# Attention stage: the values' way from PSUM to the output projection, by transposes or by DRAM scratch

## The reference, cut to what matters

```python
qkv = x @ w_qkv.T * hid ** (-0.5)          # 16 heads of 16 channels, 1024 tokens
scores = jnp.einsum('bhqd,bhkd->bhqk', q, k) * d ** (-0.5)
attn = jax.nn.softmax(scores, axis=-1) * (s / np.sqrt(s - 1.0))
out = jnp.einsum('bhqk,bhkd->bhqd', attn, v) * s ** (-0.5)
return out @ w_o.T * hid ** (-0.5)
```

## Time and profile before

| what | value |
|---|---|
| median of 3 runs | 5788.56 us (5783.28 to 5793.2) |
| profiled execution | 5800.13 us, span 5798.4 us |
| busy: TensorE, VectorE, ScalarE, GpSimd | 94%, 78%, 60%, 27% |
| pairs in the attention stage | 128, from about 2111 to 4832 us |
| DMA in the stage | 58 GB/s, 17.8% of 16 engines |

### The profile page before, as it was taken

How to read it: one execution, slowest core, us unless ns; L and a number is a source line. 1 busy time by engine, 2 the same in 40 slices (tenths; PEclk the granted TensorE clock), 3 DMA queues, 4 the chain that set the end, 5 groups by cost and what they waited for, 6 DMA issues and landing times. The chain is left out here.

```text
span 5798.4 us, 130675 instructions
## 1 busy us (share of the span) xinstructions
PE 5424.4 (94%) x50016; PEld 3657.9 (63%) x50016; DVE 4495.1 (78%) x7377; ACT 3471.6 (60%) x5278; POOL 1559.4 (27%) x2076
## 2 busy tenths in 40 slices
PE   7999757999989979999999999999999997799999
PEld 6777546999978834444444444444444444699998
DVE  6888676555547779999999999999999995755554
ACT  4555453333324548888888888888888886433332
POOL 5777544333320000111111111111111113533332
PEclk9999878999999979999999999999999998999999
DMA  1111292222218921111111111111111113222221
GB/s 51 51 51 51 72 275 97 95 86 87 85 62 313 332 96 47 60 58 58 57 58 60 58 58 57 58 60 57 58 57 58 60 51 100 77 89 85 95 93 49
DMA packets 315520, 495.78 MB, mean 86 GB/s; under 512 B 36314, under 2 KB 221028, under 8 KB 311024
## 3 DMA queue, kind: packets, MB, share of 16 engines
q1 hardware_dynamic: 289736, 424.67, 22.9%
q0 software_dynamic: 24576, 64.56, 3.4%
q10 hardware_dynamic: 808, 1.07, 0.1%
HBM read 321.82 MB, written 168.82 MB: 85 GB/s over the span
## 5 line engine op out<-in xcount | busy, mean ns | idle before, releaser
L1751 DVE TENSOR_REDUCE at_best<-at_psM 128x2 f32<-128x1024 f32 x2048 | 2431.6, 1222 | 225.1 <-PE at_psM L1808 212.0
L1707 ACT ACTIVATE at_p<-at_psE 128x1024 f32<-128x1024 f32 (+1 forms) x2688 | 2077.5, 824 | 527.8 <-PE at_psE L1824 514.1
L1824 PE MATMUL at_psE<-at_q,at_k 50*128 50x512 f32 x4096 | 1173.4, 436 | 7.6 <-ACT at_p L1707 6.4
L1808 PE MATMUL at_psM<-at_k,at_q 48*128 48x512 f32 x4096 | 1092.6, 458 | 37.2 <-DMA at_k<-scratch_qk 27.1
L1835 PE MATMUL at_psO<-at_p,at_v 128*17 128x256 f32 x16384 | 1109.1, 383 | 0.1
L1107 ACT ACTIVATE e_h_hi<-e_psH 128x512 fp32r<-128x512 f32 x512 | 306.6, 599 | 919.5 <-PE e_psH L90 770.2
L1824 PEld LDWEIGHTS at_psE<-at_q,at_k 50*128 50x128 f32 x4096 | 548.0, 185 | 462.4 <-issue 225.0
L1181 DVE SCALAR_TENSOR_TENSOR e_h_lo<-e_psH,e_h_hi 128x512 fp32r<-128x512 f32 x512 | 354.1, 692 | 601.7 <-ACT e_h_hi L1107 527.2
L1835 PEld LDWEIGHTS at_psO<-at_p,at_v 128*17 128x17 f32 x16384 | 364.0, 96 | 542.1 <-issue 349.2
L1808 PEld LDWEIGHTS at_psM<-at_k,at_q 48*128 48x128 f32 x4096 | 471.4, 185 | 312.5 <-DVE at_best L1751 146.4
L90 PE MATMUL e_psE<-e_w_hi,e_h_hi 128*128 128x256 f32 x2048 | 582.5, 284 | 0.0
(11 more groups left out here) (210 smaller groups left out, 8376.4 us busy)
## 6 DMA issues: line engine op xcount, KB each, us to landing
e_w_raw<-in_w SPq DMA_DIRECT2D x64, 1024.0 KB
scratch_qk<-cp_qkh SPq DMA_DIRECT2D x64, 512.0 KB
scratch_qk<-cp_qkl SPq DMA_DIRECT2D x64, 512.0 KB
at_q<-scratch_qk SPq DMA_DIRECT2D x256, 128.0 KB
at_k<-scratch_qk SPq DMA_DIRECT2D x252, 128.0 KB
scratch_v<-cp_va SPq DMA_DIRECT2D x32, 544.0 KB
at_v<-scratch_v SPq DMA_DIRECT2D x126, 136.0 KB, 9.6
a_x<-in_x SPq DMA_DIRECT2D x32, 512.0 KB
```

What stands on the lines that cost most here:

```text
L1707: nc.scalar.activation(P[:, u:u + n, :], src, ACT.Exp, scale=HD ** -0.5).then_inc(p_ready, 1)
L1751: nc.vector.reduce_max(best[j % 2][:, h, :, qt], psM[h][:], AX_X).then_inc(m_taken, 1)
L1808: last = nc.tensor.matmul(psM[h][:, a, :], Q[j][r, 128 * qt:128 * qt + 128], K[j][r, 512 * h:512 * h + 512], start=True, stop=True)
L1824: last = nc.tensor.matmul(psE[:, u - u0 if n == 2 else 2, :], K[j][r, 128 * kc:128 * kc + 128], Q[j][r, 512 * half:512 * half + 512], star ...
```

## The change

The values stay with channels on partitions. ScalarE's copy `OT` is stored to DRAM scratch `ot`; a unit of 128 channels x 256 tokens is read back from it, and its sums are read back beside it, each repeated over the 16 channels of its head. VectorE takes the reciprocal of all 128 x 256, GpSimd multiplies and splits as before. The six transposes a pair, the copy of `turn_out` and the normalising are gone. TensorE's order, `MAX_AT` (13) and VectorE's place (`INVERT_AT = 10`, after query 10) are new. The unit inverted in pair pp is loaded in pair pp, and there SyncE issues it after `load_pair`. The last batch's second half takes the same way with buffers of its own. x and the output are addressed in another order of the same tiles.

```diff
-        OUT_AT, MAX_AT, VALUES_AT, NORM_AT = 1, 11, 3, 3
+        OUT_AT, MAX_AT, VALUES_AT, INVERT_AT = 1, 13, 3, 10
+    rows = ot.rearrange("(b k i) a (m w) c -> b k m (i a) w c", k=2, i=4, m=4)
...
+            def store_values(p):
+                sp.wait_ge(oT_ready, p + 1)
+                sp.dma_start(ot[p].rearrange("a r c -> r a c"), OT[:].rearrange("r (a c) -> r a c", a=2)).then_inc(oT_stored, 16)
+            def load_unit(u, slot, b, k, m, needed):
+                sp.wait_ge(oT_stored, 16 * needed)
+                after(sp, ofT_ready, u - 1)
+                sp.dma_start(raw[slot][:], rows[b, k, m][:, 0:HD, :]).then_inc(unit_loaded[slot], 16)
+                sp.dma_start(den[slot][:], rows[b, k, m][:, HD:HD + 1, :].broadcast_to([8, HD, 256])).then_inc(unit_loaded[slot], 16)
...
                     load_pair(pp + 3, (pb + 3) % 4)
+                if not first(pp):
+                    store_values(pp - 1)
+                if has_turned(pp):
+                    u, k, m = turned_unit(pp, pb)
+                    load_unit(u, pb % 2, b if pb >= 4 else b - 1, k, m, PB * b + 4 if pb >= 4 else PB * b)
                 if there(pp + 1):
                     load_max(pp + 1, (pb + 1) % 4)
...
+            store_values(NP - 1)
+            sp.wait_ge(oT_stored, 16 * NP)
+            for m in range(4):
+                span = slice(256 * m, 256 * m + 256)
+                sp.dma_start(end_den[:, span], rows[B - 1, 1, m][:, HD:HD + 1, :].broadcast_to([8, HD, 256])).then_inc(end_loaded[m], 16)
+                sp.dma_start(end_raw[:, span], rows[B - 1, 1, m][:, 0:HD, :]).then_inc(end_loaded[m], 16)
...
             def split_out(u, slot, k, m, b):
-                pool.wait_ge(xo_taken, u + 1)
+                pool.wait_ge(rden_ready, u + 1)
+                after(pool, xo_lo_ready, u - 1)
+                nc.gpsimd.tensor_tensor(oT[slot][:], raw[slot][:], den[slot][:], ALU.mult).then_inc(ofT_ready, 1)
+                pool.wait_ge(ofT_ready, u + 1)
...
             def take_values(p):
-                after(act, t_done, p)
+                after(act, oT_stored, 16 * p)
-            def take_out(u, slot, bank):
-                nc.scalar.activation(oT[slot][:], bank[:, 128:384], ACT.Copy).then_inc(xo_taken, 1)
...
-            def normalise(p, pb, b):
+            def invert(u, slot):
+                dve.wait_ge(unit_loaded[slot], 32 * (u // 2 + 1))
+                nc.vector.reciprocal(den[slot][:], den[slot][:]).then_inc(rden_ready, 1)
+            def divide_end(m):
+                nc.vector.reciprocal(end_den[:, span], end_den[:, span]).then_inc(end_rden_ready, 1)
+                nc.vector.tensor_tensor(end_raw[:, span], end_raw[:, span], end_den[:, span], ALU.mult).then_inc(end_oT_ready, 1)
...
-                        if 2 * i + h == NORM_AT and not first(pp):
-                            normalise(pp - 1, (pb - 1) % PB, b if pb > 0 else b - 1)
+                        if 2 * i + h == INVERT_AT and has_turned(pp):
+                            invert(pp - 4, pb % 2)
...
-            def turn_values(p):
-            def turn_out(k, m, needed, bank):
...
+                output(), query(0, -1), key(0), query(1, 0), last_values(6)
+                query(2, 0), key(1), key(2), last_values(7)
+                key(3), query(3, 3), query(4, 3), key(4), values(pp, pb % 4, 0)
+                key(5), key(6), query(5, 6), values(pp, pb % 4, 1, (0,))
+                key(7), query(6, 7), key(8), values(pp, pb % 4, 1, (1,))
+                query(7, 8), key(9), query(8, 9), key(10), values(pp, pb % 4, 2)
+                key(11), query(9, 11), key(12), query(10, 12), next_max_rows(), values(pp, pb % 4, 3, (0,))
+                query(11, 12), key(13), key(14), values(pp, pb % 4, 3, (1,))
                 values(pp, pb % 4, 4, (0,)), key(15), query(12, 15), key(16), values(pp, pb % 4, 4, (1,))
+                key(17), query(13, 17), key(18), query(14, 18), key(19), values(pp, pb % 4, 5)
                 key(20), query(15, 20)
```

More of the change, by code:

```diff
@@ L1455, in _, with attention_stage @@
             groups(pe, NG, group)
-def attention_stage(nc, T, stage, x, qk, v, woT, out):
+def attention_stage(nc, T, stage, x, qk, v, ot, woT, out):
     N, D = x.shape
@@ L1486, in attention_stage @@
         OT = sb("oT", [128, 512], F32)
-        rden = sb("rden", [128, 2, KC], F32)
-        O = sb("o", [128, KC, D], F32)
+        raw = [sb(f"raw{s}", [128, 256], F32) for s in range(2)]
+        den = [sb(f"den{s}", [128, 256], F32) for s in range(2)]
+        end_raw = sb("end_raw", [128, S], F32)
+        end_den = sb("end_den", [128, S], F32)
         oT = [sb(f"ofT{s}", [128, 256], F32) for s in range(2)]
@@ L1599, in load_x @@
             def load_x(b, n):
-                sp.dma_start(X[n][:], row(xb, b)[n // 4, n % 4]).then_inc(x_loaded[n], 16)
+                sp.dma_start(X[n][:], row(xb, b)[n]).then_inc(x_loaded[n], 16)
             def store_out(u, b, n):
@@ L1756, in maximum @@
                                             best[j % 2][:, 1].rearrange("p a q -> p (a q)"), ALU.max).then_inc(mx_ready, 1)
-            def normalise(p, pb, b):
[L1760 to L1767, removed]
+            def invert(u, slot):
+                dve.wait_ge(unit_loaded[slot], 32 * (u // 2 + 1))
+                nc.vector.reciprocal(den[slot][:], den[slot][:]).then_inc(rden_ready, 1)
+            def divide_end(m):
+                span = slice(256 * m, 256 * m + 256)
+                dve.wait_ge(end_loaded[m], 32)
+                nc.vector.reciprocal(end_den[:, span], end_den[:, span]).then_inc(end_rden_ready, 1)
+                dve.wait_ge(end_rden_ready, m + 1)
+                nc.vector.tensor_tensor(end_raw[:, span], end_raw[:, span], end_den[:, span], ALU.mult).then_inc(end_oT_ready, 1)
             for j in range(4):
@@ L1830, in values @@
                 if kc == 0 and heads[0] == 0:
-                    after(pe, o_ready, pp)
+                    after(pe, oT_ready, pp)
                     pe.wait_ge(v_loaded[j], 16 * (pp // 4) + 16)
@@ L1901, in output, with next_max_rows @@
                         project_out(ub, n, psE[:, 2, :])
-                def turns():
+                def next_max_rows():
                     pe.wait_ge(p_ready, NG * pp + MAX_AT - 1)
-                    if has_turned(pp):
-                        u, k, m = turned_unit(pp, pb)
-                        turn_out(k, m, PB * b + 4 if pb >= 4 else PB * b, psE[:, 2, :])
                     if there(pp + 1):
                         max_rows(pp + 1, (pb + 1) % 4)
[L1912 to L1921, removed]
+                output(), query(0, -1), key(0), query(1, 0), last_values(6)
[6 more added lines that the diff above has]
+                query(11, 12), key(13), key(14), values(pp, pb % 4, 3, (1,))
                 values(pp, pb % 4, 4, (0,)), key(15), query(12, 15), key(16), values(pp, pb % 4, 4, (1,))
-                key(17), query(13, 17), query(14, 17), key(18), key(19), values(pp, pb % 4, 5)
+                key(17), query(13, 17), key(18), query(14, 18), key(19), values(pp, pb % 4, 5)
                 key(20), query(15, 20)
@@ L1929, in _ @@
             project_out(B - 2, PB - 1, psE[:, 0, :])
[L1930 to L1933, removed]
             for n in range(PB):
@@ L1955, in hybrid_kernel @@
         projection_stage(nc, T, "cp", x1, wqkv_bT, qk, v)
-        attention_stage(nc, T, "at", x1, qk, v, woT, out)
+        attention_stage(nc, T, "at", x1, qk, v, ot, woT, out)
         routing_stage(nc, T, R, "r2", out, wg)
```

43 lines of the change are left out of this document (20 added, 23 removed).

## The result

The changed kernel takes 7059.6 us, median of 4 runs (7048.6 to 7074.0), against 5788.2 us before: ratio 1.220, interval 1.2183 to 1.2217. The forecast was 6924 us in a range of 6450 to 7200. Of the 1271 us, 1136 had been forecast.

The account below looks back on a forecast made before the run. TensorE was taken to bound the attention stage, VectorE close behind; a late unit makes pairs 30.6 us, 9.3 more: 5800.1 + 1125 (121 pairs) + 10 = 6935, less 11.6 for the runs' median, 6924 us; range 6450 to 7200.

Parts of the forecast that it names:

- TensorE bound: Attention stage: TensorE bounds the 21.3 us pair, VectorE close behind; a long VectorE halt reaches TensorE after two tiles.
- The 32-partition loads at the head of the queue: SyncE's queue: these loads run on two of 16 DMA engines, so transfers behind land late; values load 9.6 us after issue.
- The order in SyncE's queue as the cause: The unit's store and loads, issued behind the nine loads, land at 22.5 us into the pair on average.
- The reciprocal: VectorE's new reciprocal of 256 columns, once a pair: between 0.42 and 2.3 us, taken as 1.8.
- TensorE's saving by the dropped transposes and the new order: TensorE's work per pair: net -0.7 us, so TensorE alone would need about 20.6 us.
- Rival A: The unit lands in time, no halt; with a reciprocal of 1.8 us about 21.4 us a pair, 5800 us; chance 0.12.
- Its other branch: Rival A with the reciprocal at its lower bound: 20.6 us a pair, 5712 us, faster; chance of faster 0.06.
- the clock's term: TensorE at half clock for 3.4 to 6.1 us behind each pair's halt: 1.1 to 2.3 us lost, 1.7 taken.
- 6.4 + 1.7: Per pair: 6.4 us from the unit's landing to the next output projection, plus 1.7 us for the lowered clock.
- the forecast 19.4: Values load of the nine: issued at 9.8 us into the pair, landing 9.6 us later, at 19.4.
- The end: Last batch's second half, after the last copy of sums: +8 us, and +2.4 for the other quarters; together +10.
- B: The unit is late but TensorE's clock holds: 28.9 us a pair, 6719 us; chance 0.17.

Follow-up runs that it names:

- e2: The changed kernel with each of the four loads onto 32 partitions split into two of 16 partitions, same place in the queue; 6309.8 us, ratio 1.0875.
- e3: The kernel before the change, with the four loads onto 32 partitions each split into two of 16 partitions; 5780.8 us, ratio 0.9979.
- e4: The changed kernel with only the two key loads onto 32 partitions split into loads of 16 partitions; 6622.6 us (one run), ratio 1.144.
- e1: The changed kernel with the raw values' store and the unit's two loads issued before the nine loads in SyncE's queue; 6076.9 us, ratio 1.0493.
- e6: e5 with VectorE's reciprocal over 16 of the 256 columns, the other 240 not inverted, for timing only; 5720.6 us, ratio 0.9883.
- e5: The changed kernel with the edits of e1 and e2 together; 5804.1 us, ratio 1.0027.
- e11: e5 with the reciprocal taken five times in a row, holding VectorE about 7 us longer with no transfer late; 6956.6 us (one run), ratio 1.202.

## Why the prediction was right

**The steps that held.** TensorE bound, VectorE close behind, and the two PSUM buffers passing a halt on: TensorE's 788.9 us of waits against the reciprocal's 774.7. The 32-partition loads at the head of the queue as what makes the rest land late: shown by e2, e3 and e4. The order in SyncE's queue as the cause: e1. The reciprocal: 1.8 us from the slope of the narrow ones, 1.753 measured; with 16 columns at 243 ns and 256 at 1743 (e6, e5) it is 6.25 ns a column. The upper bound of 2.3 was too high, and so was the estimate of 2.1 from the Trainium skill's page "VectorE: DVE Perf Modes" (section "Walkthrough: the 8-slice pipeline in each mode"). TensorE's saving by the dropped transposes and the new order: 0.7 us forecast, 0.6 seen between e6 and the kernel before. Rival A's sum for a unit in time, 21.4 us a pair and no change, is e5: 21.47 and 5804. Its other branch, a short reciprocal, 5712, is e6: 5721.

**The term that was too small.** The forecast had 30.6 us a pair, 31.8 were measured; 121 times 1.2 is 145, about what the sum missed. It is the clock's term: 1.7 us in the sum, 31.8 - 28.9 = 2.9 in the result. I took the stretch at half clock behind a halt from two halts of the routing stage, 3.4 and 6.1 us. Where the halt comes back every pair it is 7.9 us on average (4.0 to 12.2), and 6.0 in e11.

I also counted its cost only behind the landing. There it was right: from the reciprocal's start to the next projection it takes 8.1 us, which is 6.4 + 1.7. The missing 1.2 us lie ahead of it. The half clock reaches through the next projection to the last values of the pair before, on which SyncE waits for its loads. Those started at 4.9 us into the pair and now start at 6.1 on average (7.6 in the pair shown, 4016.86 to 4024.50). That pushes the landing back again: the values land at 20.9 instead of the forecast 19.4. The three transfers behind them needed somewhat less than I gave them, and the reciprocal starts at 23.7 instead of 22.5.

**A hit that was partly luck.** The halt of 7.2 us forecast and 7.24 measured is a difference of two times, and both came over 1 us late: VectorE wanted the unit at 16.4 us into the pair, not at 15.3, and got it at 23.7, not at 22.5. At full clock, in e5, the reciprocal does start at 15.15. The errors cancelled in the halt, but not in the pair.

**A slip.** The prediction has the nine loads "for the pair after next". They are for the pair three ahead, `load_pair(pp + 3)`. No term hangs on it.

**The end.** Forecast +10 us. From the last copy of sums to the stage's end it was 10.1 us (4831.9 to 4842.0), and is 24 (6094.2 to 6118.1), so +14. SyncE's store of the last values and the first reciprocal on them:

```profile
6094.92 0.37 SPq L1622 DMA_DIRECT2D scratch_ot<-at_oT  x1
...
6101.18 1.75 DVE L1797 RECIPROCAL at_end_den<-at_end_den 128x256 f32<-128x256 f32 x1 [16.85 <-DMA at_end_raw<-scratch_ot]
```

6.3 us from issue to reciprocal, against 8.7 forecast; what follows is longer than I had it.

**The rivals that fell.** A was never near in the changed kernel: the three transfers took the 10 us of the values load ahead of them, not the 3.6 to 3.8 of the stores. Once no 32-partition load stands in front, small transfers are quick: 2.1 us for the store of 256 KB in e1, 2.6 for the values load of 136 KB in e2. The Trainium skill's page "DMA: Bandwidth & Descriptors" (section "Anatomy of one DMA — SWDGE (gpsimd) path") has 2.0 us and bytes at 436 GB/s, stated for transfers that GpSimd issues; the estimates by it would be 2.6 and 2.3 us, near these but not equal to them. B, a clock that holds, is refuted: all five kernels of the table above with a late or held VectorE have time at half clock in the stage, and e5 has none.

## What to carry to other kernels

Read a transfer's time to landing from what is queued just ahead of it, not from others of its size later in the queue: here the same 136 KB took 10.0 us behind the four 32-partition loads and 2.6 behind their halves. Before a small, urgent transfer is added, list what needs to land by when and issue in that order: moving three issues gave back 983 of 1271 us, and the next transfer in line then became the late one. On an engine chain that is otherwise dense, as here, price a halt that recurs each iteration at its length plus the time at a lower clock behind it: here 1 to 3 us, for halts of 1.2 to 7.2 us. And ask what else starts late by it, such as the loads that wait for slowed work.

## What was not expected of the hardware

Halts of about 1.6 us a pair (e2; 3.1 in two pairs of eight, 1.0 in the others) were enough to bring the granted clock of the stage to 0.88, with 6.2 us a pair at half, though a single halt of 4.7 us had passed at full clock in the routing stage. In the changed kernel the half clock outlasted the halt by 7.9 us on average and by 12.2 at most, with TensorE busy, where the two halts of the routing stage had shown 3.4 and 6.1.
